# Sixteen batches of an attention block: the middle fourteen written out in place of a loop

## The chip, the core and the metric

The kernel runs on one core of a Trainium2 chip. The metric is the device time of one execution in microseconds (us). The core's engines, as the profile calls them, are PE (TensorE, matrix multiplications; its weight loads stand apart as PEld), DVE (VectorE), ACT (ScalarE), POOL (GpSimd) and SP (SyncE, which here only issues the data transfers). Each engine has an instruction stream of its own and the engines meet at semaphores: an instruction waits until a counter has reached a value, and adds to another when it is done.
## The reference

The input x has 16 batches of 512 channels and 32x32 = 1024 positions. Each batch goes through the same attention block:

```python
n = H * W                                     # 1024; HEADS = 8, HEAD_DIM = 64
qkv = jnp.einsum('bchw,oc->bohw', x, w_qkv)
q, k, v = jnp.split(qkv, 3, axis=1)           # each to (b, 8, 64, n); q times SCALE
sim = jnp.einsum('bhdi,bhdj->bhij', q, k)
attn = jax.nn.softmax(sim, axis=-1)
out = jnp.einsum('bhij,bhdj->bhid', attn, v)
y = jnp.einsum('bchw,oc->bohw', out, w_out) + b_out[None, :, None, None]
mean_sq = jnp.mean(y * y, axis=1, keepdims=True)
y = y * jax.lax.rsqrt(mean_sq + SCALE) * rms_scale[None, :, None, None]
return y + x
```

## The kernel before

**Slots and places.** A batch is cut into eight slots, one for each pair of heads and each half of the 1024 queries. A slot has 16 places in each engine's stream. At the even places PE makes the scores of one block of 128 keys for two heads (`scores`, L563 and L565), ACT takes their exponential (L647), POOL adds the results up over the blocks for the softmax's sum (L963, L967), and PE multiplies them with the values (`values`, L578). The odd places hold everything else: projections for a later slot (L433, L466), products whose maxima DVE takes (L530, L544, L808), the sums of the slot before (L509), the output projection (L490) and the normalisation of y. Every slot ends with an item called T, one small matmul that turns the maxima around (L477, tile `neg_ident`). There is one of them in each slot, so its start time marks the slots in the trace.

**Work that crosses a batch's end.** The last two key blocks of a slot, its sum and its output projection are done in the slot after it, so slot 0 of a batch finishes slot 7 of the batch before. The last part of the normalisation of y for a batch is done in slots 0 to 2 of the next (`SCALE_AT`, `INVERT_AT`, `ROOT_AT`). The streams of two batches therefore lock into each other, and no barrier stands between them.

**Who writes the order.** The order is written by hand. Each engine has a function `one(body)` that emits the eight slots of one batch, and `run_bodies` calls it: once for batch 0 (body0), once for a body that a hardware loop runs for batches 1 to 14, and once for batch 15 (bodyz). Each engine loops over its own stream and has its own loop register. A prologue projects what batch 0 needs, and an epilogue finishes batch 15.

**Waits in the loop.** Each wait is for a count that grows with the batch, for example 14 times the number of slots done. In body0 and bodyz the batch is a number of Python, so the counts are constants in the instructions. In the loop the batch is a register, and each count is first worked out by the sequencer; these are the rows `REGISTER_ALU` and `ISA` in the order, and `ALU_OP` and `FUSED_REGOPS` in the trace. `aux_counts` (L240), `Body.consumed` (L268), `claim` (L400) and `scores` (L550) are where such counts arise. The loop is L289.

Of the kernel before, what the change touches and what calls it, by code (L numbers as in the profile page):

```python
# [102 lines left out]
def attention_kernel(nc, x, wqkv, wout, bias, scale, consts, out):  # L103
# [22 lines left out]
    LOOPS = B - 2  # L126
# [4 lines left out]
    with ctx:  # L131
# [154 lines left out]
        def run_bodies(eng, one):  # L286

            one(Body(body0, 0, True, False))
            with eng.Fori(1, 1 + LOOPS) as b:  # L289
                one(Body(loop, b, False, False))  # L290
            one(Body(bodyz, B - 1, False, True))

# [17 lines left out]
        def _(sp):  # L310
# [50 lines left out]
            def one(body):  # L361
# [11 lines left out]
                if not body.last:  # L373
# [16 lines left out]
                    load_w(1)  # L390

            run_bodies(sp, one)
            finish_half(B - 1, 0)
            finish_half(B - 1, 1)
# [4 lines left out]
        def _(pe):  # L399
# [219 lines left out]
            for slot, name, _ in PRO_ITEMS:  # L619
                if name[0] != "M":  # L620
                    item(start, slot, name)
                elif name[2] == "0":
                    maxima_of_tile(start, slot, int(name[1]))
            run_bodies(pe, one)
            end = Body(epi, B, False, True)
            last = Body(epi, B - 1, False, True)
# [10 lines left out]
        def _(act):  # L637
# [129 lines left out]
            act.wait_ge(wo_set, 1)  # L767
            act.wait_ge(spill_set, 1)
            run_bodies(act, one)
            end = Body(epi, B, False, True)  # L770
            copy_sums(B * SLOTS, 0)
# [281 lines left out]
```

## Time and profile before

| | |
|---|---|
| median of 3 runs | 4476.18 us (4475.98 to 4479.22) |
| the profiled execution's own time | 4478.85 us |
| its span, first to last instruction | 4477.0 us |
| mean granted PE clock | 0.969 of full speed |
| PE busy | 4175.7 us, 93% |
| PEld busy | 2465.0 us, 55% |
| DVE busy | 2910.1 us, 65% |
| POOL busy | 2711.8 us, 61% |
| ACT busy | 2290.3 us, 51% |
| chain that ended last, by engine | PE 76%, DVE 13%, issue 7%, ACT 3% |

Durations come from one profiled execution. "Issue" is time in which an engine waited for nothing that the profile shows. A row that ends in x14 stands for fourteen instructions; where three durations stand behind it they are the least, the median and the greatest, in ns.

### The profile page before, as it was taken

The numbers are of one execution on the slowest core, as the hardware profiler recorded it, in microseconds if no ns is written. First come the engines' busy times: TensorE is split into PE (matmuls) and PEld (weight loads), VectorE is DVE, ScalarE is ACT, GpSimd is POOL, SyncE is SP. The second block draws the span as 40 slices with busy tenths as digits, with TensorE's granted clock in tenths as the row PEclk, the third lists the DMA queues.
The fourth block names the chain that finished last, engine by engine and source line by source line (L and its number), as shares of the span: only waits on it lengthen the run. The fifth ranks groups of instructions, "written<-read, shape, count | busy, mean of one in ns | idle before, by whom it ended". The sixth has DMA issues, their size and how long they took to land.

```text
span 4477.0 us, 65017 instructions
## 1 busy us (share of the span) xinstructions
PE 4175.7 (93%) x18624; PEld 2465.0 (55%) x18624; DVE 2910.1 (65%) x2796; ACT 2290.3 (51%) x3969; POOL 2711.8 (61%) x2092
## 2 busy tenths in 40 slices
PE   7999999999999999999999999899999999999997
PEld 5555555555555555555555555555555555555553
DVE  5666666666666666666676666766667666676766
ACT  3545555455554555555554554545545455455553
POOL 4566556565565655656656566655666556666666
PEclk8999999999999999999999999999999999999998
DMA  3111111111111111111011110110101101011110
GB/s 133 40 45 48 39 40 65 39 48 38 58 48 39 48 38 58 48 39 60 27 62 43 39 67 29 58 48 30 67 29 58 48 32 64 29 58 48 38 38 29
DMA packets 71453, 214.06 MB, mean 48 GB/s; under 512 B 8153, under 2 KB 8281, under 8 KB 58209
## 3 DMA queue, kind: packets, MB, share of 16 engines
q1 hardware_dynamic: 71008, 208.80, 13.3%
q8 instruction: 198, 3.24, 0.3%
q14 instruction: 247, 2.02, 0.2%
HBM read 168.92 MB, written 39.85 MB: 47 GB/s over the span
## 4 chain that ended last, share of the span: by engine, by line
PE 76%; DVE 13%; issue 7%; ACT 3%; DMA 0%; POOL 0%; DVEq 0%; ACTq 0%; SPq 0%; POOLq 0%
PE pv L578 17%; PE aux L433 16%; PE aux L466 9%; PE score L563 9%; PE aux L490 9%; PE score L565 7%; DVE maxima L808 6%; PE aux L544 4%; DVE inv_sum L852 3%; PE pv L509 3%; PE aux L530 2%; DVE k_l L802 1%; ACT k_hh L670 1%; DVE rms_b L846 1%; ACT probs L647 0%
## 5 line engine op out<-in xcount | busy, mean ns | idle before, releaser
L967 POOL TENSOR_TENSOR prob_sum<-prob_sum,probs 128x512 f32<-128x512 f32 x1536 | 1979.5, 1312 | 826.2 <-ACT probs L647 823.7
L808 DVE TENSOR_REDUCE maxima<-aux 128x1 fp32r<-128x1024 f32 x1024 | 1202.8, 1216 | 919.6 <-PE aux L544 660.5
L647 ACT ACTIVATE probs<-score 128x512 f32<-128x512 f32 x2048 | 1112.2, 594 | 1089.9 <-PE score L565 1016.1
L578 PE MATMUL pv<-probs,v_sb 128*64 128x512 f32 x4096 | 997.5, 608 | 0.0
L563 PE MATMUL score<-q_hl,k_hh 128*128 128x512 f32 x2048 | 891.9, 435 | 40.6 <-issue 27.0
L565 PE MATMUL score<-q_hm,k_l 72*128 72x512 f32 x2048 | 821.5, 401 | 0.0
L963 POOL TENSOR_TENSOR prob_sum<-probs 128x512 f32<-128x512 f32 x256 | 338.7, 1344 | 795.9 <-ACT probs L647 795.9
L433 PE MATMUL aux<-x_hi,w_ring 128*128 128x512 f32 x2048 | 678.8, 413 | 51.3 <-DVE maxima L808 39.6
L563 PEld LDWEIGHTS score<-q_hl,k_hh 128*128 128x128 f32 x2048 | 390.6, 191 | 328.7 <-issue 198.6
L578 PEld LDWEIGHTS pv<-probs,v_sb 128*64 128x64 f32 x4096 | 249.1, 136 | 485.7 <-issue 421.7
L466 PE MATMUL aux<-w_ring,x_hi 128*128 128x256 f32 x2048 | 429.7, 310 | 89.3 <-DVE maxima L808 89.3
L433 PEld LDWEIGHTS aux<-x_hi,w_ring 128*128 128x128 f32 x2048 | 364.3, 192 | 209.2 <-DVE maxima L808 121.3
L852 DVE RECIPROCAL inv_sum<-inv_sum 128x256 f32<-128x256 f32 x256 | 440.3, 1736 | 9.0 <-ACT inv_sum L700 5.9
L466 PEld LDWEIGHTS aux<-w_ring,x_hi 128*128 128x128 f32 x2048 | 354.4, 213 | 142.7 <-DVE maxima L808 104.1
L565 PEld LDWEIGHTS score<-q_hm,k_l 72*128 72x128 f32 x2048 | 393.2, 192 | 63.8 <-issue 7.2
L433 PE MATMUL aux<-x_lo,w_ring 128*128 128x512 f32 x1024 | 405.8, 396 | 0.0
L466 PE MATMUL aux<-w_ring,x_lo 128*128 128x256 f32 x1024 | 310.7, 303 | 0.0
L831 DVE TENSOR_TENSOR y_sb<-y_sb,aux 128x1024 f32<-128x1024 f32 x192 | 234.5, 1222 | 95.2 <-PE aux L490 84.2
L802 DVE TENSOR_TENSOR k_l<-aux,k_hh 64x512 fp32r<-64x512 f32 x256 | 175.9, 687 | 181.5 <-ACT k_hh L670 179.6
L544 PEld LDWEIGHTS aux<-k_hh,q_hm 64*128 64x128 f32 x762 | 112.4, 185 | 311.3 <-issue 235.2
L544 PE MATMUL aux<-k_hh,q_hm 64*128 64x512 f32 x762 | 278.1, 444 | 1.2
L544 PE MATMUL aux<-k_hh,q_hl 64*128 64x512 f32 x762 | 277.7, 444 | 0.0
(72 smaller groups left out, 4524.2 us busy)
## 6 DMA issues: line engine op xcount, KB each, us to landing
w_ring<-w_split SPq DMA_DIRECT2D x93, 1024.0 KB, 4.8
x_stage<-x SPq DMA_DIRECT2D x128, 256.0 KB, 4.6
resid<-x SPq DMA_DIRECT2D x128, 256.0 KB, 5.8
out<-resid SPq DMA_DIRECT2D x128, 256.0 KB, 2.0
w_split<-w_ring SPq DMA_DIRECT2D x3, 1024.0 KB, 11.9
w_split<-y_sb SPq DMA_DIRECT2D x3, 1024.0 KB, 3.8
y_sb<-wqkv SPq DMA_DIRECT2D x4, 512.0 KB, 8.5
probs<-wqkv SPq DMA_DIRECT2D x2, 512.0 KB, 7.9
```

Of the source, the lines that this page charges most:

```text
L433: last = pe.matmul(out_ap, w[:, wp, k, cols], xp[:, k, xcols], start=(k == 0 and n == 0), stop=(k == KT - 1 and n == 2))
L466: last = pe.matmul(bank(k)[:, i * WCOLS:(i + 1) * WCOLS], xp[:, c, jt * P:(jt + 1) * P], w[:, wp, c, :], start=(n == 0), stop=(n == 3 * KT ...
L490: last = pe.matmul(bank(k + i), w[:, pair, m * P:(m + 1) * P], o[:], start=(n == 0), stop=(n == 2))
L544: last = pe.matmul(bank(k + h), q_hi_at(nhalf, e, h, it), k_hh[rows, npair % 2, e, h * HALF:(h + 1) * HALF], start=True, stop=True)
L563: pe.matmul(score[e][:], k_hh[:, pair % 2, e, keys], q_hl[:, half, e, :], start=True, stop=False)
L565: pe.matmul(score[e][:], k_l1[0:D + 2 * IT, pair % 2, e, keys], q_hm[0:D + 2 * IT, half, e, :], start=False, stop=True).then_inc(score_rea ...
L578: pe.matmul(pv[half][e * D:(e + 1) * D, :], v_sb[:, pair // 2, j, (pair % 2) * P + e * D:(pair % 2) * P + (e + 1) * D], probs[:, j % 4, e, ...
L647: act.activation(probs[:, j % 4, e, :], score[e][:], ACT.Exp, scale=SOFT).then_inc(prob_ready, 1)
L808: dve.tensor_reduce(maxima[:, n:n + 1], bank(k, 2), AX_X, ALU.max).then_inc(aux_free[k], 1)
L852: dve.reciprocal(inv_sum[:, cols], inv_sum[:, cols]).then_inc(inv_ready, 1)
L963: pool.tensor_tensor(prob_sum[:, e, :], probs[:, 0, e, :], probs[:, 1, e, :], ALU.add).then_inc(prob_added, 1)
L967: pool.tensor_tensor(prob_sum[:, e, :], prob_sum[:, e, :], probs[:, j % 4, e, :], ALU.add).then_inc(prob_added, 1)
```

## The change

The hardware loop over batches 1 to 14 becomes a loop of Python that runs while the program is built. The body is emitted fourteen times, each time with the batch as a number.

```diff
@@ -286,7 +286,7 @@
         def run_bodies(eng, one):
 
             one(Body(body0, 0, True, False))
-            with eng.Fori(1, 1 + LOOPS) as b:
+            for b in range(1, 1 + LOOPS):
                 one(Body(loop, b, False, False))
             one(Body(bodyz, B - 1, False, True))
```

PE's stream, the place where one middle batch passes into the next. Before, the end of the loop's body (T is L477, then the rest of a projection):

```order
L404 REGISTER_ALU
L477 MATMUL aux<-neg_ident,maxima 128x128
L433 MATMUL aux<-x_hi,w_ring 128x512 x2
L433 MATMUL aux<-x_lo,w_ring 128x512
L433 MATMUL aux<-x_hi,w_ring 128x512 x2
L433 MATMUL aux<-x_lo,w_ring 128x512
L289 REGISTER_ALU
L289 COMPARE_AND_BRANCH
```

The branch leads back to the start of the loop's body, where the first scores and the last two key blocks' values of the batch before stand:

```order
L289 ISA
L556 ISA
L563 MATMUL score<-q_hl,k_hh 128x512
L565 MATMUL score<-q_hm,k_l 128x512
L559 ISA
L563 MATMUL score<-q_hl,k_hh 128x512
L565 MATMUL score<-q_hm,k_l 128x512
L575 ISA
L578 MATMUL pv<-probs,v_sb 64x512
L575 REGISTER_ALU
```

Now, the same place on PE between batch 1 and batch 2:

```order
L477 MATMUL aux<-neg_ident,maxima 128x128
L433 MATMUL aux<-x_hi,w_ring 128x512 x2
L433 MATMUL aux<-x_lo,w_ring 128x512
L433 MATMUL aux<-x_hi,w_ring 128x512 x2
L433 MATMUL aux<-x_lo,w_ring 128x512
L563 MATMUL score<-q_hl,k_hh 128x512
L565 MATMUL score<-q_hm,k_l 128x512
L563 MATMUL score<-q_hl,k_hh 128x512
L565 MATMUL score<-q_hm,k_l 128x512
L578 MATMUL pv<-probs,v_sb 64x512 x4
L509 MATMUL pv<-prob_sum,ones_d 64x512 x2
```

The branch and the register rows are gone; the matmuls stand in the same order with the same operands.

DVE's stream at the end of the loop's body before (the last sum of squares of the first half, L867):

```order
L864 REGISTER_ALU
L866 ISA
L867 TENSOR_TENSOR sq_a<-sq_a,rms_b 128x512
L289 REGISTER_ALU
L289 COMPARE_AND_BRANCH
```

And now, where a middle batch begins, with that sum as its first row:

```order
L867 TENSOR_TENSOR sq_a<-sq_a,rms_b 128x512
L867 TENSOR_TENSOR sq_a<-sq_a,sq_b 128x512
L808 TENSOR_REDUCE maxima<-aux 128x1 x2
L852 RECIPROCAL inv_sum<-inv_sum 128x256
L802 TENSOR_TENSOR k_l<-aux,k_hh 64x512 x2
```

DVE goes from one batch's last operation straight to the next batch's first. ACT, POOL and SP change in the same way. PE's stream as built has 2641 such rows before and 12578 now, DVE's 563 and 1853.

## Rows read from the trace of the kernel before

**Rows 1.** The page: span, and busy time of the engines.

```profile
span 4477.0 us, 65017 instructions
PE 4175.7 (93%) x18624; PEld 2465.0 (55%) x18624; DVE 2910.1 (65%) x2796; ACT 2290.3 (51%) x3969; POOL 2711.8 (61%) x2092
```

**Rows 2.** Line 289: engine, operation, count, ns min/median/max, first and last start.

```profile
L289 PEldq FUSED_REGOPS  x14: 50/50/50, 315.5 to 3919.4; - x14
...
L289 PEldq COMPARE_BRANCH  x14: 82/3608/3865, 585.7 to 4189.3; - x14
...
L289 DVEq COMPARE_BRANCH  x14: 55/63/63, 589.5 to 4193.1; - x14
```

**Rows 3.** Timeline of PE, the T matmul at nine slot ends: start, duration.

```profile
151.42 0.22 PE L477 MATMUL aux<-neg_ident,maxima 128*128 128x128 f32 x1
...
315.69 0.22 PE L477 MATMUL aux<-neg_ident,maxima 128*128 128x128 f32 x1
349.82 0.22 PE L477 MATMUL aux<-neg_ident,maxima 128*128 128x128 f32 x1
...
421.73 0.22 PE L477 MATMUL aux<-neg_ident,maxima 128*128 128x128 f32 x1
...
485.60 0.22 PE L477 MATMUL aux<-neg_ident,maxima 128*128 128x128 f32 x1
...
585.86 0.22 PE L477 MATMUL aux<-neg_ident,maxima 128*128 128x128 f32 x1
...
4189.49 0.22 PE L477 MATMUL aux<-neg_ident,maxima 128*128 128x128 f32 x1
4224.05 0.22 PE L477 MATMUL aux<-neg_ident,maxima 128*128 128x128 f32 x1
...
4359.75 0.22 PE L477 MATMUL aux<-neg_ident,maxima 128*128 128x128 f32 x1
```

**Rows 4.** Timeline of PE behind the first branch back (585.7 us).

```profile
589.75 0.50 PE L563 MATMUL score<-q_hl,k_hh 128*128 128x512 f32 x1 [2.23 <-issue]
...
596.36 1.97 PE L509 MATMUL pv<-prob_sum,ones_d 128*64 128x512 f32 x4 [3.55 <-issue]
```

**Rows 5.** Timeline of PE behind the last branch, which isn't taken (4189.3 us).

```profile
4191.14 0.47 PE L563 MATMUL score<-q_hl,k_hh 128*128 128x512 f32 x1
...
4194.14 1.03 PE L509 MATMUL pv<-prob_sum,ones_d 128*64 128x512 f32 x4
```

**Rows 6.** Waits, 585.8 to 600 us: us in total, times, longest.

```profile
DVE sq_a L867 <- issue: 5.9, 1, 5.9
```

**Rows 7.** Waits of PE from 585.8 to 4189.4 us.

```profile
PE pv L509 <- issue: 33.7, 12, 4.1
PE score L563 <- issue: 27.0, 13, 2.3
```

**Rows 8.** Waits in batch 0, 59 to 315.6 us: the longest wait for issue.

```profile
PEld score L563 <- issue: 9.4, 24, 1.0
```

**Rows 9.** Windows: stretch, length, busy per engine, then PEclk, DMA share, GB/s.

```profile
585.86:620.00 34.14, 27.00 (x100) 14.58 (x99) 22.22 (x23) 16.47 (x28) 13.36 (x12) 0.89 0.20 65
4189.40:4224.00 34.60, 32.85 (x137) 18.15 (x136) 29.61 (x29) 21.16 (x35) 20.07 (x16) 1.00 0.18 62
```

**Rows 10.** DMA queues, batch 0 (59 to 315.6 us): packets, MB, share.

```profile
q8 instruction: 9, 0.15, 0.2%
q14 instruction: 7, 0.06, 0.1%
```

**Rows 11.** DMA queues, 585.8 to 600 us.

```profile
q14 instruction: 7, 0.06, 1.8%
q8 instruction: 2, 0.03, 1.1%
```

**Rows 12.** Register arithmetic of lines 554 and 265, as rows 2.

```profile
L554 PEldq ALU_OP  x1764: 32/32/32, 319.7 to 4184.9; - x196
...
L265 DVEq ALU_OP  x1400: 40/40/47, 322.0 to 4189.8; - x175
```

## The prediction

> **What bounds the kernel now.** I read the page first. PE is busy 93% of the span and no other engine passes 65% [rows 1]; the reader is to see that a gain must come out of the few per cent in which PE stands, or out of a lower clock. Then I asked for line 289, the loop. Its rows say three things [rows 2]. PE enters the loop at 315.5 us. It comes to its branch fourteen times, first at 585.7 and last at 4189.3 us. The branch takes 3608 ns in the median but 82 ns at least; fourteen passes need thirteen branches back, and the last falls through. So going back looks dear and going on cheap. The third view is the list of PE's waits within the loop. The rows "issue", in which PE waited for nothing that the profile shows, are 27.0 us in 13 waits before the first scores and 33.7 us in 12 waits before the sums [rows 7]: about one of each for every branch back. On DVE one wait for issue of 5.9 us stands behind the first branch [rows 6].
>
> What an edge costs as a whole must be read from the same work with and without it, since the waits of several engines lie beside each other. The T matmul ends each slot, so the distance of two of them is a slot's or a batch's length [rows 3].
> - Batch 1 is the first pass through the loop, with no branch back before it: 585.86 - 315.69 = 270.17 us.
> - Batches 2 to 14 each begin behind a branch back: (4189.49 - 585.86) / 13 = 277.20 us.
> - The difference is 7.03 us. Both run the same instructions from the same place of the program; only the way in differs.
>
> The seven us can be followed. Behind the first branch back the scores begin at 589.75 and the sums (L509) at 596.36, so 10.50 us lie between T and the sums [rows 3, 4]. In batch 15, which follows the branch that is not taken, they begin at 4191.14 and 4194.14, 4.65 us behind T [rows 3, 5]. That is 5.85 us, of which PE's two issue waits are 2.23 + 3.55 = 5.78. The rest comes after: the sums then take 1.97 us for four records in place of 1.03. The granted clock over the first 34 us of the batch is 0.89 in the one case and 1.00 in the other [rows 9], so for some of that stretch PE ran at 1.2 in place of 2.4 GHz; what it did before was to stand for 2.2 and 3.6 us. I take the stalls as the cause and the lower clock as their consequence, so both go together.
>
> Why it stalls: in the 14 us behind the branch back nine packets of the kind "instruction" land, while the whole of batch 0, 256.6 us, has 16 [rows 10, 11]. The engines refetch code at the edge and wait for it.
>
> **The change part by part.**
>
> 1. Thirteen branches back go, on each of five engines: 13 x 7.03 = 91.4 us less. All of it lies on the path that sets the end, because it is measured as a batch's length on PE and not as a sum of stalls. Adding PE's own issue waits gives 27.0 + 33.7 = 60.7 us; the remaining 31 us are clock and waits for DVE and ACT, which also refetch. As a check by batch 15, whose constants are those of the new code: its slots 0 to 4 take 4359.75 - 4189.49 = 170.26 us, those of batch 1 take 485.60 - 315.69 = 169.91 [rows 3]. Its slot 0, 4224.05 - 4189.49 = 34.56 us, stands beside batch 1's 349.82 - 315.69 = 34.13. Neither has a branch back before it, and they agree within 0.4 us.
>
> 2. The register arithmetic goes. On PE line 554 has 1764 operations of 32 ns, on DVE line 265 has 1400 of 40 ns [rows 12], which is 100 per batch and 4.0 us of DVE's sequencer. Were all of DVE's on the path it would be 14 x 4.0 = 56 us more gain. The nearest rows say otherwise. Batch 15 with constants takes 0.35 us longer over five slots than batch 1 with registers (above). Slots 3 to 7 of batch 0, constants, take 315.69 - 151.42 = 164.27 us and those of batch 1, registers, 585.86 - 421.73 = 164.13 [rows 3]; this half has the loads of x in it. So the sequencers run ahead of their engines and hide this work, and I take 0. The ends that these rows give are a loss of 0.35 + 0.14 = 0.5 us per batch, 7 us in all, and on the other side the same 7 us; the 56 us stay as a far bound with little chance, because a tenth of it would already show as 0.4 us per batch of the wrong sign here.
>
> 3. The code gets long and each piece is read once. Before, the body's code was fetched anew behind each branch back [rows 11]; now it comes in sequence throughout. Batch 0 is such a straight piece, and its longest wait for issue is 1.0 us, in a row of weight loads of 24 waits [rows 8]; no wait like the 2.2 and 3.6 us of the edge stands there. I take 0. If the cover fails, a late page costs PE from 2.2 us, the issue wait before the scores, to 7.0 us, the whole edge.
>
> 4. SP loses its branch and its counts. Its transfers are issued behind the same semaphores in the same order, and I find no wait that would move, so 0. What is late next once the edge is gone is what stands in batch 1's slot 0 already, DVE's maxima and reciprocals in the middle of the slot, and that is inside the 270.17.
>
> The sum against the profiled execution: 4478.85 - 91.4 = 4387.5 us. That execution lies 2.7 us above the median of the runs, so the same subtraction from the median gives 4384.8. I take 4386.
>
> **Rivals.**
>
> A. The branch itself is all that goes, and the 7 us belong to slot 0 of a batch whatever leads to it. For it: slot 0 carries the work that crosses the batches. Against it: batch 1 and batch 15 have this work too and need 34.13 and 34.56 us. It would give the branch's shortest duration alone, 13 x 0.08 = 1.1 us less: 4475 to 4478 us, no change. The Trainium skill, "Advanced Engine Details and Errata", section "Control Flow Timing", puts a compare-and-branch at about 108 ns; by that the gain would be 1.4 us and the change pointless. The trace has something near it for the branch that falls through, 82 ns, and 3.6 us for PE's others [rows 2]. "Runtime: NRT & Kernel Launch" of the Trainium skill, section "Instruction fetch mechanics", limits the figure: a taken branch out of the fetched pages has to wait for its code, for which it gives no time. By that rule the whole 91.4 us may go.
>
> B. Straight code also stalls, though less: some pages arrive late because five streams fetch at once, or because the new streams stand elsewhere against the data transfers. A third of the gain lost, 30 us, needs thirteen late pages at 2.2 us. This gives 4405 to 4465 us. Batch 0 and 15 speak against it, but they are two short pieces near the ends.
>
> C. Slower. Fetching decides: in fourteen written-out batches with some 16 instruction packets each, one in sixteen comes so late that all engines stall as at an edge. One such stall per batch costs 14 x 7.03 = 98.4 us, which is 7 us more than is won; this is the point where it turns (4486). Two per batch would give 4478.85 - 91.4 + 196.8 = 4584 us. Against it: in batch 0 none of its 16 packets did that [rows 8, 10].
>
> D. The gain is greater, since some of the register arithmetic lay on DVE's part of the path: 15 to 56 us beyond the forecast, 4330 to 4370 us. Against it are the comparisons in part 2.
>
> **How the numbers follow.** Forecast 0.87, A 0.02, B 0.05, C 0.03, D 0.03. The forecast's own range is the 7 us of part 2 to each side, some 6 us for where the clock falls in the new batches (0.43 us between the two slots 0 that have no edge, times thirteen), and 3 us between profiled and timed runs: together up to 16 us, 4370 to 4402. I widen the upper end by a few us for the near part of B, to 4406. By 0.2%, about 9 us, a measurement of this kernel can tell a change from none. Faster by more than that are the forecast, B and D, 0.95; A is within, 0.02; C is slower, 0.03.
>
> **What would show each step right or wrong.** In the profile of the changed kernel no line 289 has a branch, and the issue waits of PE before L563 and L509, longer than 1 us, are gone, with DVE's before L867. T to T over each middle batch is 269 to 271.5 us, with all slots 0 near 34.4. The granted clock over the first 34 us of a middle batch is above 0.95. Slots 3 to 7 keep their length; were they shorter, part 2 is wrong and D right. Instruction packets come evenly, without the cluster of nine. If new issue waits of 2 us or more stand inside the batches, part 3 is wrong and B or C holds. If slot 0 stays at 41 us without a branch, part 1 is wrong and A holds.

## The result and the profile after

| | before | after |
|---|---|---|
| median of 4 runs | 4477.0 us (4475.98 to 4479.22) | 4379.0 us (4377.06 to 4379.9) |
| the profiled execution's own time | 4478.85 us | 4379.61 us |
| span | 4477.0 us | 4377.8 us |
| mean granted PE clock | 0.969 | 0.979 |

The ratio is 0.978, with a 95% interval from 0.9763 to 0.9797. The kernel is 98.0 us faster. The forecast was 4386 us, in a range from 4370 to 4406.

The written-out kernel was timed in this set of runs only. In the three later sets the median of the kernel before was 4482.34, 4472.81 and 4473.76 us, so a difference below that is taken against 4379.0 is uncertain by some 5 us either way. Where the difference of two traces is given, each trace is one execution and has its part in that spread.

The page of the changed kernel, its span, its busy times and its instruction queues:

```profile
span 4377.8 us, 52968 instructions
...
PE 4137.0 (94%) x18624; PEld 2440.6 (56%) x18624; DVE 2912.8 (67%) x2796; ACT 2284.7 (52%) x3969; POOL 2712.5 (62%) x2092
...
q8 instruction: 152, 2.49, 0.2%
q14 instruction: 108, 0.88, 0.1%
```

The counts of matmuls and of operations on DVE, ACT and POOL are those of [rows 1]. The 12,049 instructions that are missing belong to the sequencers: the register arithmetic is gone, and some more plain waits stand in its place. PE's busy time fell by 38.7 us although it does the same matmuls, and the mean granted clock rose from 0.969 to 0.979. Of instruction packets 260 land (152 + 108), where 445 did before:

```profile
q8 instruction: 198, 3.24, 0.3%
q14 instruction: 247, 2.02, 0.2%
```

PE's T matmul at the end of batch 0, of slot 2 of batch 1, of batch 1 and of batch 14 (start, duration), which answers to [rows 3]:

```profile
314.18 0.22 PE L477 MATMUL aux<-neg_ident,maxima 128*128 128x128 f32 x1
...
419.46 0.22 PE L477 MATMUL aux<-neg_ident,maxima 128*128 128x128 f32 x1
...
583.50 0.22 PE L477 MATMUL aux<-neg_ident,maxima 128*128 128x128 f32 x1
...
4088.81 0.22 PE L477 MATMUL aux<-neg_ident,maxima 128*128 128x128 f32 x1
```

Batches 2 to 14 take (4088.81 - 583.50) / 13 = 269.64 us each, where they took 277.20: 7.56 us less, 98.3 us in all. Batch 1 takes 269.32 in place of 270.17 us. These two make up 99.1 of the 99.2 us between the two profiled executions. Single batches lie between 269.0 and 270.4 us, where batches 2 to 14 lay between 272.5 and 281.9. Nearly all of the gain is in slot 0, whose mean over these batches fell from 41.58 to 34.41 us.

The whole stretch of batches 2 to 14 (length, busy per engine, PEclk, DMA share, GB/s), before and then after:

```profile
585.86:4189.49 3603.63, 3388.08 (x15134) 2000.96 (x15133) 2352.74 (x2263) 1859.99 (x3224) 2190.62 (x1691) 0.97 0.14 47
```

```profile
583.50:4088.81 3505.31, 3349.42 (x15133) 1977.65 (x15132) 2353.86 (x2263) 1854.47 (x3224) 2191.38 (x1692) 0.98 0.13 47
```

The length less PE's busy time is the time in which PE stood: 215.6 us before, 155.9 after. So the 98.3 us are 59.7 us of standing and 38.7 us in which the same matmuls took longer.

The first 34 us of batch 2 (length, busy per engine, PEclk, DMA share, GB/s), against the first row of [rows 9]:

```profile
583.49:617.90 34.41, 32.64 (x138) 18.16 (x136) 29.43 (x29) 21.17 (x35) 19.87 (x17) 1.00 0.17 62
```

In the same stretch of time PE now finishes 138 matmuls in place of 100, and the granted clock is 1.00 in place of 0.89. All waits of PE over batches 2 to 14 follow, and behind them its waits for DVE and ACT over the same batches before (those for issue are [rows 7]):

```profile
PE aux L466 <- DVE maxima L808: 70.6, 78, 3.3
PE aux L490 <- DVE maxima L808: 36.6, 36, 1.8
PE aux L433 <- DVE maxima L808: 35.9, 78, 1.3
PE score L563 <- ACT probs L647: 7.0, 26, 0.3
PE aux L544 <- DVE k_l L802: 1.1, 7, 0.2
```

```profile
PE aux L466 <- DVE maxima L808: 75.2, 78, 3.4
PE aux L490 <- DVE maxima L808: 38.2, 36, 1.9
...
PE aux L433 <- DVE maxima L808: 31.4, 69, 1.2
...
PE score L563 <- ACT probs L647: 9.1, 26, 0.4
```

The two rows "issue" with 27.0 and 33.7 us are gone. What is left are waits for DVE and a few for ACT, 151.2 us together, where they were 153.9. Of instruction packets one lands from 583.5 to 598 us, where nine did behind the branch [rows 11]:

```profile
q14 instruction: 1, 0.01, 0.3%
```

### The profile page after: what moved, and what is told of

Read it like the earlier page. It is cut to its first block, busy times and chain, and to the rows that moved or that the text cites. A ratio compares the mean times of both kernels' runs of the same rounds, so it can differ in the third digit from the quotient of the medians.

```text
span 4377.8 us, 52968 instructions
## 1 busy us (share of the span) xinstructions
PE 4137.0 (94%) x18624; PEld 2440.6 (56%) x18624; DVE 2912.8 (67%) x2796; ACT 2284.7 (52%) x3969; POOL 2712.5 (62%) x2092
## 4 chain that ended last, share of the span: by engine, by line
PE 76%; DVE 17%; issue 4%; ACT 2%; POOL 0%; DMA 0%; DVEq 0%; POOLq 0%; SPq 0%
PE pv L578 17%; PE aux L433 17%; PE aux L466 9%; PE aux L490 9%; PE score L563 8%; DVE maxima L808 8%; PE score L565 7%; PE aux L544 4%; DVE inv_sum L852 3%; PE pv L509 2%; DVE k_l L802 2%; PE aux L530 2%; ACT k_hh L670 1%; DVE rms_b L846 1%; DVE sq_a L867 1%
## 5 line engine op out<-in xcount | busy, mean ns | idle before, releaser
L433 PE MATMUL aux<-x_hi,w_ring 128*128 128x512 f32 x2048 | 674.0, 411 | 60.0 <-DVE maxima L808 44.3
L466 PE MATMUL aux<-w_ring,x_hi 128*128 128x256 f32 x2048 | 428.5, 309 | 84.4 <-DVE maxima L808 84.4
L433 PEld LDWEIGHTS aux<-x_hi,w_ring 128*128 128x128 f32 x2048 | 361.6, 191 | 222.8 <-DVE maxima L808 90.0
L466 PEld LDWEIGHTS aux<-w_ring,x_hi 128*128 128x128 f32 x2048 | 353.0, 212 | 137.7 <-DVE maxima L808 137.7
L433 PE MATMUL aux<-x_lo,w_ring 128*128 128x512 f32 x1024 | 404.9, 395 | 0.0
L466 PE MATMUL aux<-w_ring,x_lo 128*128 128x256 f32 x1024 | 310.6, 303 | 0.0
```

Of the source, the lines that this page charges most:

```text
L433: last = pe.matmul(out_ap, w[:, wp, k, cols], xp[:, k, xcols], start=(k == 0 and n == 0), stop=(k == KT - 1 and n == 2))
L466: last = pe.matmul(bank(k)[:, i * WCOLS:(i + 1) * WCOLS], xp[:, c, jt * P:(jt + 1) * P], w[:, wp, c, :], start=(n == 0), stop=(n == 3 * KT ...
```

## The experiments

The first question was whether the branch back or the register arithmetic had cost the time, the second what a branch back costs by, the third which engine's branch it is. Unless a diff says otherwise it is against the kernel before, inside `run_bodies`. Lines moved by an edit are named in the text.

### Half the branches back

```diff
-            with eng.Fori(1, 1 + LOOPS) as b:
-                one(Body(loop, b, False, False))
+            with eng.Fori(1, 1 + LOOPS // 2) as i:
+                one(Body(loop, 2 * i - 1, False, False))
+                one(Body(loop, 2 * i, False, False))
```

> The loop stays on every engine but its body holds two batches, so there are seven passes and six branches back in place of thirteen; nearly all register arithmetic stays. Theory (each branch back costs (4477.0 - 4379.0) / 13 = 7.5 us, the arithmetic nothing): 4379 + 6 x 7.5 = 4424 us, and batches of about 277 and 270 us in turn. Rival (the waits with register counts cost the time, 98 / 14 = 7 us per batch): 4477 us, as before.

Measured: 4425.45 us (4423.15 to 4428.21), ratio to before 0.9867 (0.9843 to 0.9891). Its branches on PE, and PE's waits for issue:

```profile
L289 PEldq COMPARE_BRANCH  x7: 83/3579/3793, 852.4 to 4138.3; - x7
```

```profile
PE pv L510 <- issue: 12.6, 6, 3.1
PE score L564 <- issue: 12.6, 6, 2.3
```

Six waits of each kind belong to six branches back (L564 and L510 are the scores and the sums). The time is 46.5 us above the written-out kernel, 7.7 us for each. From T to T the six batches behind a branch back take 274.2 to 278.8 us; of the other eight, six take 269.4 to 270.3 and two 273.1. The rival's 4477 us is ruled out.

### Registers, but no branch back

```diff
-            with eng.Fori(1, 1 + LOOPS) as b:
-                one(Body(loop, b, False, False))
+            for i in range(1, LOOPS):
+                with eng.Fori(i, i + 2, 2) as b:
+                    one(Body(loop, b, False, False))
+            one(Body(loop, LOOPS, False, False))
```

> Batches 1 to 13 are written out, but each stands in a hardware loop of a single pass, so its counts are still worked out in registers and its compare-and-branch is never taken back; batch 14 has constants. Theory (the branches back cost all): 4379 us, at most 2 us more for thirteen branches that fall through. Rival (register counts cost the time): 4470 us or more.

Measured: 4384.34 us (4383.63 to 4385.74), ratio 0.9777 (0.9753 to 0.9801). Thirteen branches are there and none is taken back:

```profile
L290 PEldq COMPARE_BRANCH  x13: 74/74/95, 585.7 to 3824.8; - x13
```

This lies 5.3 us above 4379.0, no more than the uncertainty of that comparison, and 3.3 us above what was expected at most. In the traces batches 2 to 14 take 3508.68 us (T at 585.82 to T at 4094.50), 3.4 us more than written out, and 2.7 of these are one batch of 272.3 us. So the arithmetic with its thirteen branches holds a twentieth of the 98 us by these numbers, and can't be told from nothing.

### The loop with a hint to fetch

```diff
-            with eng.Fori(1, 1 + LOOPS) as b:
+            with nc.Fori(1, 1 + LOOPS, engines=type(mybir.ALL_ENGINES)([eng.engine]), hint_back_edge=True) as b:
                 one(Body(loop, b, False, False))
```

```profile
L289 PEldq BRANCH_PREFETCH_HINT  x14: 36/36/45, 312.9 to 3819.3; - x14
...
L289 PEldq COMPARE_BRANCH  x14: 88/357/454, 583.1 to 4088.6; - x14
```

The branch's median went from 3608 to 357 ns, and PE has no wait for issue left between 580 and 4088 us. Batches 2 to 14 take 3505.43 us, 0.1 us more than written out, and 289 instruction packets land in place of 445. The forecast of this run was too careful: the second wait, before the sums, goes with the first. All that this kernel adds to the one before is the hint, so what cost was that the code behind the branch was not there; the branch taken and the registers are still in it.

### PE alone loops

```diff
-            with eng.Fori(1, 1 + LOOPS) as b:
-                one(Body(loop, b, False, False))
+            if eng is nc.tensor:
+                with eng.Fori(1, 1 + LOOPS) as b:
+                    one(Body(loop, b, False, False))
+            else:
+                for b in range(1, 1 + LOOPS):
+                    one(Body(loop, b, False, False))
```

> PE alone keeps the hardware loop; the other four engines are written out. Theory (PE's own refetch makes its two waits, 60.7 us in all, and the rest of the 98 us comes from DVE's and ACT's): about 4440 us. Rival (the waits of the engines lie beside each other and PE's alone makes the whole edge): 4477 us. Rival (DVE's refetch of 5.9 us is what counts and PE's is hidden behind it): under 4400 us.

Measured: 4479.09 us (4467.87 to 4484.92, 10 runs) beside 4482.34 us for before, ratio 0.9989 (0.9975 to 1.0003). PE's waits for issue before the sums and the scores (L513 and L567 here):

```profile
PE pv L513 <- issue: 42.8, 13, 4.1
...
PE score L567 <- issue: 26.6, 13, 2.3
```

Batches 2 to 14 in its trace:

```profile
585.87:4193.76 3607.89, 3383.70 (x15133) 1999.92 (x15132) 2355.18 (x2263) 1855.47 (x3224) 2190.97 (x1691) 0.97 0.13 46
```

PE's branch alone makes the whole edge. PE stands 69.4 us for its code, and the thirteen batches are 102.6 us longer than written out: it stood 68.3 us more and was busy 34.3 us more with the same matmuls. The theory's 4440 us is wrong, and so is the second rival's "under 4400 us".

### All but PE loop, and DVE alone loops

The edits are the one above with `if eng is not nc.tensor:` and with `if eng is nc.vector:`.

> The opposite of the run in which PE alone looped: PE is written out, the other four engines keep the hardware loop. Theory now (PE's refetch makes the edge and what the others refetch lies beside it, but not all of it once PE comes on time): behind a branch back DVE begins its next L867 5.9 us late, so its first maxima would be done about 12.2 us behind T against 7.6 us without, and PE waits for them at its next projection: up to 4.6 us per edge, 60 us in all, 4439 us. Rival (PE's refetch is the only one that matters): 4379 us.

> DVE alone keeps the hardware loop, all others are written out. If DVE's late maxima are what costs when PE is straight: the same as with four looping engines, up to 4439 us. If the cost there is ACT's or POOL's: 4379 us.

Measured: all but PE 4470.97 us (4465.01 to 4477.69), ratio 0.9995 (0.9985 to 1.0005); DVE alone 4467.14 us (4465.36 to 4469.16), ratio 0.9988 (0.9979 to 0.9998). DVE's one late stretch of code costs 88 us above 4379.0 with nothing else late (88.2 us over batches 2 to 14 in the trace), and ACT, POOL and SP add some 3.8 us to it, between two medians of one set of runs. The timeline of DVE behind the first branch back, with DVE alone looping (the sum of squares is L871, the maxima L812):

```profile
588.38 0.69 DVE L871 TENSOR_TENSOR sq_a<-sq_a,rms_b 128x512 f32<-128x512 f32 x1
595.01 0.69 DVE L871 TENSOR_TENSOR sq_a<-sq_a,sq_b 128x512 f32<-128x512 f32 x1 [5.94 <-issue]
595.73 2.35 DVE L812 TENSOR_REDUCE maxima<-aux 128x1 fp32r<-128x1024 f32 x2
```

And PE, in the same stretch:

```profile
597.01 1.22 PE L437 MATMUL aux<-x_hi,w_ring 128*128 128x512 f32 x2 [5.10 <-DVE maxima L812]
```

The waits over the whole program, of which thirteen are DVE's for its code:

```profile
PE aux L437 <- DVE maxima L812: 107.2, 95, 5.9
...
DVE sq_a L871 <- issue: 79.5, 13, 6.7
```

DVE waits 5.94 us for its code and comes 4.9 us late to its maxima (11.10 us behind T, where the written-out kernel has 6.16). They free the bank for PE's next projection, and PE stands 5.10 us. The wait before L437 is 107.2 us, where it is 44.3 before L433 in the written-out kernel: 62.9 us more, or 4.8 per edge. So the 4.6 us per edge and the 60 us in all were read nearly right as waits. What was left out is that the same matmuls then take longer: the two behind the wait take 1.22 us, where the same form takes 0.73 at the next projection (607.34 us), and over batches 2 to 14 PE is busy 25.4 us more than written out, with 62.8 us more of standing. In the kernel before, PE's late code hid all of this, since PE itself came to the place 5.8 us late.

### ACT alone loops

The edit is the same with `if eng is nc.scalar:`.

> ACT alone keeps the hardware loop. In the trace of before ACT has pauses of 3.3 us and of 3 to 5.5 us in the 12 us behind the branch back, part of which were waits for PE. Theory: the first exponentials of the batch come about 2 us late, PE's values wait for them, at most 3 us per edge: 4379 to 4418 us. Rival (ACT's code arrives while it has nothing to do): 4379 us.

Measured: 4382.74 us (4379.74 to 4385.22), ratio 0.9799 (0.9783 to 0.9816).

```profile
ACT probs L651 <- issue: 35.2, 13, 3.1
```

The exponentials are L651 here. ACT stands 2.7 us per edge for its code, and the program is 3.7 us longer for thirteen of them, which is less than the uncertainty of the comparison. PE's wait for the exponentials shows how little of the 35.2 us reaches it: 20.0 us in all, where the written-out kernel has 9.6.

```profile
PE score L567 <- ACT probs L651: 20.0, 50, 1.1
```

### PE stands twice, and no code is fetched

The edit is against the written-out kernel. SP issues two small transfers in the memory outside the core, and PE waits for each:

```diff
                     sp.wait_ge(aux_full[k], n + 1)
+                    if c == VB and 2 <= b <= LOOPS:
+                        sp.dma_start(stand[0], bias).then_inc(stand_over, 16)
+                        sp.wait_ge(pv_done, 128 * b)
+                        sp.dma_start(stand[1], bias).then_inc(stand_over, 16)
                     load_w(c)
...
+                if slot == 0 and 2 <= body.b <= LOOPS:
+                    pe.wait_ge(stand_over, 16 * (2 * (body.b - 2) + 2))
                 pe.wait_ge(prob_added, 14 * done)
...
+                    if slot == 0 and j == 0 and e == 0 and 2 <= body.b <= LOOPS:
+                        pe.wait_ge(stand_over, 16 * (2 * (body.b - 2) + 1))
```

> The written-out kernel with no branch anywhere. At the head of batches 2 to 14 PE waits twice, before its first scores and before its sums, each time for a transfer of 2 KB that SP issues when PE is done with what stands before. Each should make PE stand for about 2 us, where the branch back made it stand 2.1 and 2.8 us in the mean, and no code is refetched. Theory (the price of an edge is PE standing there, with the lower clock that follows): the batches get longer by more than the two waits themselves, about 7.5 / 4.7 times 4 us = 6.4 us per batch, 4379 + 83 = 4462 us. Rival (what follows the waits at an edge, 2.8 us, is due to the other engines' refetch, not to PE having stood): the waits alone, 4 us per batch, 4431 us.

Measured: 4452.35 us (4450.66 to 4455.91), ratio to before 0.9956 (0.9939 to 0.9973). The waits of PE:

```profile
PE pv L517 <- DMA stand<-bias: 25.3, 13, 2.1
PE score L573 <- DMA stand<-bias: 24.9, 13, 2.0
```

The sums are L517 and the scores L573 here. Batches 2 to 14 as a whole, and the first 34 us of batch 2:

```profile
585.08:4165.57 3580.49, 3376.47 (x15133) 1994.74 (x15132) 2353.98 (x2263) 1854.87 (x3224) 2190.47 (x1692) 0.98 0.13 46
585.08:619.20 34.12, 28.69 (x114) 16.45 (x112) 24.15 (x25) 19.21 (x32) 15.56 (x13) 0.95 0.18 63
```

The waits are 50.2 us, 3.9 per batch, and the thirteen batches are 75.2 us longer than without them (73.3 us between the medians). That is 1.50 us for each us that PE stood for the transfers. With PE alone looping it was 102.6 / 69.4 = 1.48. So the surplus at an edge needs no second cost of the fetch. It comes with PE having stood there, also where no code is late. The rival's sum, the waits alone, would be 4429 us. In batch 2 the granted clock, 0.95, is between the 0.89 of the edge and the 1.00 without one.

The rows also tell the clock from a chain of further waits. Beside the written-out kernel PE stands 48.1 us more over these batches and is busy 27.1 us more, with the same matmuls. The standing is no more than the two waits themselves, so no chain of waits follows them, and the surplus is busy time at a lower granted clock (0.942 in the mean of slot 0 of these batches, in place of 1.000). In the kernel with PE alone looping it is the same: 68.3 us of standing, 34.3 us of busy time. The spread is smaller than that: in the five traces without PE's or DVE's code late, PE is busy from 3339.7 to 3349.4 us over these batches.

### The hint on PE and DVE alone

```diff
-            with eng.Fori(1, 1 + LOOPS) as b:
+            hint = eng in (nc.tensor, nc.vector)
+            with nc.Fori(1, 1 + LOOPS, engines=type(mybir.ALL_ENGINES)([eng.engine]), hint_back_edge=hint) as b:
                 one(Body(loop, b, False, False))
```

> The hardware loop on all engines, with the fetch hint on PE and DVE alone. Theory now (PE's and DVE's late code each make nearly the whole edge, side by side; ACT alone cost 3.7 us over the program, POOL and SP nothing): 4379 + 4 = 4383 us, up to 4390. Rival (POOL, which was never tried alone, or ACT and POOL together cost as much as DVE once the other two are on time): 4440 us or more.

Measured: 4388.73 us (4380.15 to 4391.39), ratio 0.9811 (0.9791 to 0.9832). This lies within what was expected, and the rival's 4440 us is ruled out. The late code of ACT, POOL and SP together is worth the 9.7 us above 4379.0, give or take the uncertainty of that comparison. POOL was never tried alone.

### What is late next

Against the written-out kernel:

```diff
-ADD_SQUARE_AT = (((7, 14), (7, 15), (0, 0)), ((1, 1), (1, 2), (1, 3)))
+ADD_SQUARE_AT = (((7, 14), (7, 15), (0, 0)), ((1, 1), (1, 5), (1, 6)))
```

> The written-out kernel with two additions of squares on DVE moved from places 2 and 3 of slot 1 to places 5 and 6, behind the maxima. In the trace of the changed kernel PE stands 3.27 us in slot 1 before L466 until DVE has taken a maximum, which stood behind these two additions (0.92 + 1.34 to 1.58 us in DVE's row). If DVE's order is the bound there, the wait falls by about 2.9 us per batch and some of the lower clock behind it goes: 14 x 2.9 = 41 us and up to 20 more, 4320 to 4345 us. Rival (the maxima move up, but the normalisation or the sum for R comes late and makes PE wait instead): 4370 to 4390 us.

Measured: 4327.61 us (4326.23 to 4329.3), ratio to before 0.9672 (0.9652 to 0.9691). It beats both kernels, the written-out one by 51 us, and lies in the range of its forecast. The waits of PE over the whole program:

```profile
PE aux L466 <- DVE maxima L808: 39.3, 94, 1.5
PE aux L498 <- DVE sq_a L867: 21.2, 17, 3.6
```

The wait before L466 was 84.4 us in the written-out kernel, with 3.3 us as the longest. The wait for the sum of squares, 6.9 us there, grew to 21.2, which is the rival's mechanism at a smaller price. The rest of the gain is again busy time: PE is busy 4115.8 us in this kernel and 4137.0 in the written-out one.

## Why the prediction was right, step by step

**The edge (part 1): right, its size 7% low.** The price of a branch back was taken as 277.20 - 270.17 = 7.03 us; it is 7.56. The term that was off is the 270.17, a single batch. In its slot 1, from the T at 349.82 [rows 3] to the one at 388.37 us, batch 1 ran at a lower clock than the same slot of the written-out kernel (before, then after):

```profile
349.82:388.37 38.55, 34.94 (x161) 21.61 (x160) 27.52 (x25) 20.74 (x35) 24.96 (x19) 0.91 0.08 28
```

```profile
348.57:386.16 37.59, 34.11 (x160) 20.92 (x159) 27.13 (x25) 20.74 (x35) 24.75 (x19) 0.95 0.08 29
```

The work is the same, the clock 0.91 against 0.95 and the length 0.96 us more, which is more than the 0.85 us by which batch 1 as a whole was too long. Thirteen times the 0.53 us by which 270.17 exceeds 269.64 are 6.9 us. With the 0.85 us of batch 1 they make up 7.7 of the 7.9 us by which the profiled execution came out under the 4387.5 of the sum. Batch 1 has no branch back ahead of it in any kernel; where the squares are left in their place it took from 269.3 to 270.3 us in the eleven traces, so one batch is good to about 1 us, and thirteen times that is more than the error here.

**Where the seven us come from: half right.** That the engines refetch code and wait for it holds; the hint shows it. That the 31 us beyond PE's issue waits were "clock and waits for DVE and ACT, which also refetch" holds for the clock and fails for the waits. Of the 98.3 us, 60.7 are the issue waits and 37.6 the rest. PE's waits for DVE and ACT fell by 2.7 us, and its busy time by 38.7, so the rest is the clock. With PE alone looping the surplus is there as well, though no other engine refetches. DVE's late code would cost 88 us by itself and cost nothing that could be seen beside PE's; ACT's would cost 4. The thirteen branches "on each of five engines" made one cost, which PE and DVE each keep up side by side. Taking away PE's alone gives nothing, and neither does taking away those of all the others.

**Register arithmetic (part 2): right.** Zero was taken, with 7 us to each side; the kernel with registers and no branch back gives 5.3 us between the medians and 3.4 us between the traces, neither of which can be told from nothing. Slots 3 to 7 kept their length: in batch 1 164.13 us before and 583.50 - 419.46 = 164.04 after.

**Long code (part 3): right.** Among the waits of PE's matmuls over batches 2 to 14, shown above, there is none for issue, and with that rivals B and C fall. DVE's wait before L867, 74.1 us over the program before, is gone too, and so is the cluster of nine packets.

**SP and what is late next (part 4): right in kind.** DVE's maxima are what PE waits for now. That they could be moved for 51 us more was not seen from slot 0; the wait stands in slot 1.

**Rival A** would have kept slot 0 long and the time unchanged. It falls by the result: without the branch slot 0 of batches 2 to 14 takes 34.3 to 34.7 us, where it took 38.7 to 44.4. **Rival D** put the gain 15 us or more beyond the forecast, from the arithmetic; the 7 us that did come are in the length taken for batch 1, as above.

## What to carry to other kernels

Where a list of waits shows waits for issue behind a hardware loop's branch back, and instruction packets land there, find the same batch with and without a branch back ahead of it and take the difference of their lengths: that is what the loop costs, and it contains what no list of waits adds up to. Before writing the loop out, try the hint that fetches the branch's target; here it gave the same time with a program a fifth as long on PE. When two engines are late at the same place, mending one alone shows nothing, so test each alone in a kernel in which all others are on time.

## What the runs showed of the hardware

- A branch back holds PE's sequencer 3.6 us in the median, 357 ns with the hint, and 82 ns where it falls through. On DVE the branch is listed with 63 ns [rows 2], and still its next operation waits 79.5 / 13 = 6.1 us for issue in the kernel where DVE alone loops: there the wait stands behind the branch and not in it, so the branch's own duration does not tell what it costs. In the 14 us behind PE's branch back the data transfers of the batch's head land as well (720 packets, 2.10 MB); whether the code comes later for them was not tested.
- With one hint at the head of the body the later waits went too, PE's 2.8 us before the sums among them. Whether the hint alone brings that code, or the sequence then runs on ahead of PE, was not tested.
- One us of PE standing at the head of a batch cost 1.48 us of time with PE's code late and 1.50 with a transfer to wait for. With DVE's code late it was 88.2 / 62.9 = 1.40, and with all engines looping 98.3 / 60.7 = 1.62. What came on top was PE's busy time at a lower granted clock, with two stands of 1.9 us each enough for it (0.95 over the first 34 us of batch 2, in place of 1.00). Busy times that differ by up to 10 us between like traces leave these quotients uncertain by a tenth or two.
